# Output product ahead of the next batch's transposes, lows ahead of the norm, in the MLP stage of a one-core block kernel

## The reference

```python
h  = _layernorm(x, ln2_g, ln2_b)                          # x: what the mixer left
x  = x + gelu(h @ mlp_W1 + mlp_b1, approximate=False) @ mlp_W2 + mlp_b2
x  = x_in + ga * x                                        # residual of the whole block
h2 = _layernorm(x) * (1 + cb) + sb                        # second, modulated norm
gate = h2 @ gate_w                                        # router: 8 logits a row
weights, sel = top_k(gate, k=2)                           # then the experts
```

## Time and profile before

| what | value |
|---|---|
| median of three runs | 2289.16 us (2287.65 to 2293.46) |
| the profiled execution's own time | 2284.92 us |
| its span, first to last instruction | 2282.8 us |
| TensorE matmul busy | 1963.1 us, 86% |
| VectorE busy | 1416.2 us, 62% |
| ScalarE busy | 964.0 us, 42% |
| GpSimd busy | 995.2 us, 44% |
| granted TensorE clock, mean | 0.907 of 2.4 GHz |

### The profile page before, as it was taken

One profiled execution on the slowest core, in us unless ns is written; L12 is line 12 of the kernel. 1 busy time (PEld: TensorE's weight loads), 2 busy tenths in 40 slices (PEclk: granted clock), 3 DMA queues, 4 the chain that ended last, 5 costly groups with the idle time before them and its releaser, 6 DMA issues. The chain is left out here.

```text
span 2282.8 us, 57727 instructions
## 1 busy us (share of the span) xinstructions
PE 1963.1 (86%) x19628; PEld 1571.1 (69%) x19629; DVE 1416.2 (62%) x3577; ACT 964.0 (42%) x1734; POOL 995.2 (44%) x1131
## 2 busy tenths in 40 slices
PE   4888888898889888988788898885199999999997
PEld 2667766777767666777465566664188888888886
DVE  5556555555555555564588888887166666666665
ACT  3233333332233333332554554453066556566564
POOL 4122221122122221222267777776456666666664
PEclk7899988898899888989898988887599999999999
DMA  3122112100111111101344433332235544454453
GB/s 123 58 52 51 51 51 51 48 22 31 51 51 51 51 51 51 34 26 38 111 134 135 133 120 109 119 124 86 66 71 89 93 94 88 93 91 91 94 88 61
DMA packets 155520, 172.90 MB, mean 76 GB/s; under 512 B 35140, under 2 KB 136199, under 8 KB 155328
## 3 DMA queue, kind: packets, MB, share of 16 engines
q1 hardware_dynamic: 101248, 96.90, 15.0%
q0 software_dynamic: 36352, 56.78, 13.1%
q10 hardware_dynamic: 17856, 18.37, 2.3%
HBM read 109.40 MB, written 53.99 MB: 72 GB/s over the span
## 5 line engine op out<-in xcount | busy, mean ns | idle before, releaser
L1877 POOL DMA_INDIRECT out<-experts_y,experts_entry x144 | 237.3, 1648 | 191.8 <-DVE experts_y L1853 164.7
L672 PE MATMUL mixer_pv<-w_V,mixer_prob 128*128 128x33 f32 x2048 | 254.3, 280 | 13.0 <-DVE mixer_on L914 13.0
L672 PEld LDWEIGHTS mixer_pv<-w_V,mixer_prob 128*128 128x128 f32 x2048 | 241.7, 194 | 26.3 <-DVE mixer_on L914 13.9
L886 DVE TENSOR_REDUCE w_mx<-mixer_sc 128x8 bf16<-128x1024 f32 x128 | 156.0, 1219 | 92.1 <-PE mixer_sc L636 91.6
L1818 DVE TENSOR_SCALAR experts_v<-experts_v 128x512 f32<-128x512 f32 x144 | 73.9, 513 | 219.6 <-ACT experts_v L1792 204.0
L1792 ACT ACTIVATE experts_g<-experts_pg,x_b 128x256 f32<-128x256 f32 x288 | 120.9, 471 | 180.0 <-PE experts_pv L131 180.0
L1867 POOL DMA_INDIRECT experts_rows<-scratch_xs,experts_entry x144 | 169.4, 1177 | 59.8 <-issue 43.3
L799 ACT ACTIVATE mixer_prob<-mixer_sc 128x1024 f32<-128x1024 f32 x128 | 130.9, 1022 | 148.6 <-PE mixer_sc L662 148.6
L1007 POOL TENSOR_TENSOR mixer_x<-mixer_mix,mixer_hres 128x256 f32<-128x256 f32 x64 | 46.5, 726 | 314.9 <-DVE mixer_mix L868 314.0
L129 PE MATMUL experts_pg<-experts_xT,x_w 128*128 128x256 f16 x576 | 158.2, 275 | 10.2 <-issue 6.9
L1492 POOL DMA_INDIRECT scratch_queue<-mlp_entry,mlp_slot x128 | 141.1, 1102 | 50.5 <-issue 38.2
(11 more groups left out here) (364 smaller groups left out, 5820.1 us busy)
## 6 DMA issues: line engine op xcount, KB each, us to landing
mixer_x<-in_x SPq DMA_DIRECT2D x16, 512.0 KB, 4.0
w_Kz<-mixer_Kt SPq DMA_DIRECT2D x64, 128.0 KB, 2.4
mixer_hres<-mixer_h SPq DMA_DIRECT2D x16, 512.0 KB, 4.8
scratch_xs<-scratch_mod SPq DMA_DIRECT2D x16, 512.0 KB, 9.4
scratch_x<-mixer_x SPq DMA_DIRECT2D x16, 512.0 KB, 2.9
mlp_xa<-scratch_x SPq DMA_DIRECT2D x16, 512.0 KB, 4.2
mlp_stage<-in_x_w SPq DMA_DIRECT2D x16, 512.0 KB, 4.3
mlp_xb<-scratch_x SPq DMA_DIRECT2D x16, 512.0 KB
```

Of the source, the lines that this page charges most:

```text
L672: last = pe.matmul(pvO[:, i, :], prob[:, n % 2, at:at + P], V[:, n, i, :], start=True, stop=True)
L886: dve.tensor_reduce(mx[:, s % 2, :].rearrange("p (h r) -> p h r", h=2)[:, :, 0:4], sc[:, 0:2, :].rearrange("p h (j k) -> p h j k", j=4), A ...
L1877: pool.indirect_dma_start(out=out, out_offset=bass.IndirectOffsetOnAxis(ap=entry[:, s, t, 0:1].bitcast(I32), axis=0), in_=y[:, s % 2, t, : ...
```

## The change

Three lists are reordered. No instruction is added or removed, and none computes anything else.

On TensorE `transpose_rows(b - 2)` and `project(b, 0)` now stand ahead of `transpose_x(b + 1)`. On ScalarE `copy_rows(b - 2)` stands ahead of `x_parts(b + 1)`. On VectorE the low parts of chunks 4 to 7 stand ahead of `norm_x1(b + 1)`, and `add_x1(b, 0)` ahead of `low_x(b + 1)`.

```diff
@@ TensorE body
-                if not last:
-                    transpose_x(b + 1)
                 if behind >= 2:
                     transpose_rows(b - 2)
                 for t in range(TT):
                     project(b, t)
+                    if t == 0 and not last:
+                        transpose_x(b + 1)
@@ ScalarE body
+                if behind >= 2:
+                    copy_rows(b - 2)
                 if not last:
                     x_parts(b + 1)
-                if behind >= 2:
-                    copy_rows(b - 2)
@@ VectorE body
-                if not last:
-                    norm_x1(b + 1)
                 for c in range(FMC):
                     if c not in POOLED:
                         dve.wait_ge(hid_hi.sem, hid_hi.at(b, c + 1))
                         dve.tensor_tensor(hd[1][:, c, :], hid[:, c % HB, :], hd[0][:, c, :], ALU.subtract
                                           ).then_inc(hid_lo.sem, 1)
+                if not last:
+                    norm_x1(b + 1)
                 if behind >= 1:
                     scale_x2(b - 1)
+                add_x1(b, 0)
                 if not last:
                     low_x(b + 1)
-                add_x1(b, 0)
```

## The result

The changed kernel took 2300.8 us (median of 5 runs, 2299.41 to 2302.25) against 2289.17 us for the kernel before: 1.0041 of its time, 95% interval 1.0029 to 1.0052. It is slower by 12 us where 22 us less were forecast. The prediction had the wrong sign, and the time lies outside its range.

A forecast was written before the change was run, and what follows sets the result against it. VectorE with its 2.47 us of waits on other engines was taken as the loop's period. Gains of 1.25 + 0.59 = 1.84 us over 12 bodies made 22.1 us: 2267 us against 2289.16, range 2255 to 2281.

The forecast's parts named there:

- The 1.96 us are gone: VectorE's first sum in each loop body: its 1.96 us wait for product 0 disappears, with 2.5 us of cover.
- a new wait of 0.79 us appears: VectorE at the low part of the transposed input (L1426): waits 0.79 us at full clock, 1.64 at half.
- the third sum's wait: VectorE's 0.51 us wait for product 2 goes too, worth 0.59 us a body with the overlap.
- D: Rival: norm or low part held another 1.5 us, 0 to 0.5 us a body left, 2283 to 2289 us; chance 0.10.
- The period: Loop body between weight splits: 28.9 us forecast, from 30.71 us before.
- TensorE's wait before L1167: Input transposes' 4.16 us wait for the norm falls apart; no wait there over 1.5 us.
- ScalarE's row copies: Their 1.93 us run right behind the casts and hide in ScalarE's 3.48 us of idle time.
- the twelve bodies: Body 3 and the loop bodies each gain 1.84 us, 22.1 us in all; other bodies put at nothing.
- Rival B: TensorE's clock still falls in the reordered stretch; a body gains only 0.99 us, 2277 us; chance 0.16.
- Contention: GpSimd's tensor operations against VectorE: 0.9 us a body lost or 0.7 gained; taken as zero.
- priced at 0.9 us a body more: Shared SBUF interfaces of GpSimd and VectorE: by this rule alone the moved lows lose 0.9 us a body, giving 2278.

The follow-up runs named there:

- late occasion: Unedited changed kernel run where TensorE's signals come late inside GpSimd's indirect DMAs: 2300.8, 2301.0 and 2298.1 us.
- prompt occasion: Unedited changed kernel run where TensorE's signals come within 0.02 us of the matmul's end: 2263.2 and 2263.1 us.
- the kernel before with the groups: Kernel before with GpSimd's eight indirect DMAs of a body split into four, two and two: 2290.13 us, 1.0002 of the kernel before.
- the kernel with the groups of four, two and two: Changed kernel with GpSimd's eight indirect DMAs a body split into three groups, the later two behind residual tiles: 2274.44 us, 0.9929 of the kernel before.
- TensorE's part alone: Changed kernel with VectorE's order put back as before, TensorE's and ScalarE's reorder kept: 2280.22 us, then 2312.24 us unedited on another occasion.
- the kernels without the DMAs: GpSimd's indirect DMAs left out of both kernels: changed kernel 2229.21 us, kernel before 2258.56 us.
- half of them: Changed kernel with four indirect DMAs a body instead of eight: 2241.66 us, 0.9793 of the kernel before.
- five and three: Changed kernel with five indirect DMAs where all eight stood, three behind the first residual tile: 2259.43, 2261.71 and 2262.16 us.

## Why the prediction was wrong

The step that failed is this one: "Product 0 thus ends at about 1375.6, and the first sum ... does not wait. The 1.96 us are gone; product 0 has 2.5 us of cover." Its size was right. On the late occasion of the trace product 0 ended 2.2 us ahead of VectorE (1350.61 against 1352.82). What I took for granted is that an instruction's end releases whoever waits for it. The signal came 5.0 us later, and a wait of 2.78 us stood where I had put none.

The second step fell with it: "a new wait of 0.79 us appears" at the low part of the input. The input transposes' signal was late by 3.6 us, and the wait was 1.62 us. Together 2.78 + 1.62 - 0.89 = 3.51 us. In the body shown 0.21 and 0.68 us at the next two sums come to them, where the clock had fallen, and VectorE is busy 0.84 us less than on a prompt occasion (25.37 against 26.21). That makes 3.56 us, and the body's 32.44 us lie 3.61 above the prompt 28.83. In the body before it, at the full clock, the same two waits are 2.89 and 1.62 us and VectorE is busy 1.08 us less: 2.54 us, and it lies 2.60 above. Over the loop the periods differ by 31.59 - 28.83 = 2.76 us, 27.6 us of the 37.6 between 2300.8 and 2263.2; the bodies at either end of these periods lose as well (1.8 in body 3, 2.3 in body 4, 3.4 in the last one).

The row that told it was among those on which the prediction rests. The earlier trace rows end with ScalarE's L1252 and "2.40 <-remote". I used its 1.93 us and passed over the bracket, because nothing waited for that copy. It said that a signal of TensorE can be 2.4 us late there. The last body of the same trace had it for product 0 itself, with the wait of 2.08 us shown above. The rival that follows from it moves product 0 and the input transposes into the same stretch. Worked out now from before: its DMAs end at 1380.24 (1377.82 + 2.42), and signals held until then put the shift at 1380.24 + 1.53 (1376.94 - 1375.41) + 0.57 + 0.1 + 1.20 = 1383.6 instead of 1381.70. Less the 0.51 us of the third sum's wait, which takes up part of it, that is 1.4 us a body lost; the periods lost 0.9. So a loss could have been priced from the rows at hand, though not foreseen with certainty: in the same trace the input transposes' signals pass in time inside the DMAs. Of my rivals D was nearest ("the wait only changes its name"), but it had neither the place nor the price.

Where signals are prompt, the other steps stand. The period: forecast 28.9, measured 28.83 and 28.88 us. The wait at L1426: forecast 0.79, measured 0.89. TensorE's wait before L1167: forecast under 1.5, measured 0.76. The first sum's wait: none, as forecast. ScalarE's row copies: hidden. The total: forecast 2267, measured 2263.2 and 2263.1, with 10 x 1.87 = 18.7 us from the ten periods, 1.7 from body 4 and 2.7 from body 3: 23.1 us for the twelve bodies, forecast 22.1. Against the kernel before on the same occasions the gain was 27.1 and 23.3 us; the surplus of the first was not followed up. The last body is 2.8 us shorter as well (24.52 against 27.36), but there the trace of before is a late one, and the kernel before with the groups, on a prompt occasion, has 24.04: no gain of the change is shown in it.

Rival B (the clock falls): on a prompt occasion the granted clock is 1.00 through the body, so "TensorE: Matmul & The Clock Gate" of the Trainium skill, with its swing after frequent short idle spells, is not seen there. On the late occasion of the result it is 1.00 in seven of the ten periods and 0.89, 0.95 and 0.89 in the other three; in the body shown it fell at 1354.3, after TensorE had stood 0.90, 0.76, 0.32 and 1.11 us between 1347 and 1354. So the clock is a follower here: the periods at full clock are no better than 31.4 us. Contention was put at nothing, and on the prompt occasions the period came within 0.1 us (VectorE busy 26.21 us, before 26.37). The rule of "GPSIMD Engine Reference" (Key points) in the Trainium skill, priced at 0.9 us a body more, does not show here; in the kernel with the groups of four, two and two VectorE is busy 1.4 us longer, which fits it, but no run isolates it.

Open is what makes an occasion late or prompt. It is not the program (TensorE's part alone: 2280 and 2312 us, the changed kernel: 2263 and 2298 us), nor the chip alone (chip 9 was both). One thing goes with it: on late occasions many of the records of semaphore changes are missing (between 1100 and 1580 us, of some 1860 to 2040 changes by TensorE, VectorE and ScalarE, 321 to 410), on prompt ones hardly any (0 to 18). Every run here was recorded, so whether the recording takes part in the holding could not be told. The Trainium skill ("NOTIFIC — the notification-queue block", Overflow: three behaviours, one of which stalls the engine) says that the block that takes such records holds up their producers when its inner stages fill; no run here shows that it is the cause.

Not tried on a late occasion: the kernels without the DMAs, half of them, and the kernel before with the groups. That the DMAs hold the signals, and not something else that GpSimd or the occasion does in that stretch, thus rests on the place of the late signals and on the two kernels with groups. And why the hold lets some signals pass is open.

## What to carry to other kernels

Where the trace shows an instruction standing on "remote" after its producer is done, note in which stretch, and before you move anything into that stretch price the same delay for its signal, even if nobody waits for it today.

Keep signals that the pace depends on out of the stretch in which GpSimd issues a row of indirect DMAs, or cut the row so that it ends before they are due: five and three instead of eight gave 0.986 to 0.989 of the kernel before on both kinds of occasion (2259 to 2262 us), where the eight in a row gave 0.989 on one and 1.003 to 1.005 on the other. And when a kernel does not repeat its own time, run the same text again on other occasions before explaining either value.

## What the runs showed of the hardware

TensorE's signals came up to 6.6 us after the last matmul's end while GpSimd issued indirect DMAs, on four of seven occasions, and within 0.02 us on the other three. The first signal inside the stretch often passed (product 1's, 0.3 us into a group, was prompt in each body of the grouped kernels), later ones were held. Some were let go inside the row, the last ones 0 to 1.5 us after its last DMA. In two bodies of the first late trace TensorE itself slowed down clearly while signals were held: in the body shown its last two input transposes started at 1352.56 and 1353.97, 1.4 us apart, where all eight took 1.09 us on a prompt occasion. What holds the signals is not known.
